# Steps of VectorE reordered and handed to ScalarE while a graph network builds its adjacency

## The chip, the cores and the metric

One core of one Trainium2 chip runs the whole program. The metric is the time on the device for one execution, in microseconds (us). A core has engines that run side by side, each through its own list of instructions in order: TensorE (PE in the profile; its weight loads are PEld), VectorE (DVE), ScalarE (ACT), GpSimd (POOL) and SyncE (SP), which here only issues transfers. They wait for one another by semaphores.

## The reference

625 nodes with 256 features, 10,625 edges sorted by their end node `dst`. Two graph layers, each behind a layer norm and a ReLU, are added to x:

```
h = relu(layernorm(x))
for l in 0, 1, 2:                                   # edge convolution, mean over the incoming edges
    m = concat(h[dst], h[src] - h[dst]) @ W_l + b_l
    h = relu(segment_sum(m, dst) / max(count, 1))
x = x + concat(h, h1, h2, h3) @ Wf + bf
h = relu(layernorm(x));  a = segment_sum(edge_weight * (h @ W)[src], dst) + bias
x = x + relu(batchnorm(a) * gamma + beta)
```

All sums over edges go through two 625 x 625 matrices: the number of edges from s to d, and the sum of their weights. The first part of the kernel builds both; the rest multiplies by them.

## The kernel before, in words

**Tiles.** The edges are cut into 85 tiles of 125. For each tile t, `src_hot` (L583 on VectorE, L933 and L936 on ScalarE) is a one-hot matrix, 125 edges by 626 nodes: VectorE makes it in one comparison with `edge_cols`, ScalarE in two steps, the distance |node - src| and then relu(1 - distance). `dst_hot` holds, for 17 tiles at a time (a group c), the one-hot of the end nodes in a narrow window of 28: `plain_window` (L572) makes it, and `weighted_window` (L579) multiplies it by the high and the low part of the scaled edge weights (`weight_parts`). As the edges are sorted, the window moves with the tile.

**Placing.** TensorE takes the tiles in order and multiplies `src_hot` of a tile (its weights, 128 nodes s at a time) by the tile's window (L1272). The results are block r of the end nodes (125 of them), in five banks, one for each block s of source nodes. Block 0 is done piece by piece, five matmuls a tile, and between its pieces stand other jobs at fixed places (L1276 to L1292): `turn_h0(b)` turns the normalized rows of node block b, `turn_vecs` turns the bias vectors, `neighbour_terms_0` multiplies h by W0's lower half. The dictionary `jobs` (L1250) says before which piece each `turn_h0` stands. The blocks 1 to 4 go in two halves: the first half of the pieces for the banks s = 0 to 4, then the second half for the banks. In front of the first half of bank s, TensorE waits for `parts_copied` of block r - 1, bank s (L1297), that is for ScalarE to have emptied the bank. Behind block 0 come the rest of `neighbour_terms_0`, behind block 1 `own_terms_0` (L1189, four results that ScalarE reads), behind block 2 and inside block 4 the row counts (`sum_counts`, L1244). Then come `sums_0` and the layers. Block r uses the tiles 0 to 18, 15 to 35, 32 to 52, 49 to 69 and 66 to 84. Its second half begins with tile 9, 25, 42, 59 or 75.

**Who makes which tile.** `SCALAR_EARLY`, `SCALAR_NEXT` and `SCALAR_LATER` (L65) name the tiles of ScalarE: 0 and 4 before the normalization, 22 and 27 among the normalized rows, and 34 and 38, 52, 71 behind its copies of block 0, 1 and 2. The other 77 are VectorE's, in order, in the loop from L622; `src_hot` has 36 slots, so that tile t waits for the placing of tile t - 36. Other work of VectorE stands at fixed tiles of the loop: the next group's windows two tiles before a group ends (L628), the copy of the bias vectors and the cast of `degree_r` at `VECS_AT`, the low parts u_lo at 30, 38 and 42, the difference of W0's halves at 33, the flag at 62.

**The first steps.** TensorE turns the edge rows and weight rows into columns, in the banks "edges", "weights" and "parts". VectorE takes from them `rel` (L565, the end node within its window), `edge_cols` (L567) and `weight_parts` (L604). L606 to L614 reduce to `dev_max`: how far an edge lies outside its window, and whether the two parts give the weight exactly; if not, a slow general way is taken later. Then come the statistics of x (L536, L542), `weighted_window(0)`, and `scale_shift` (L545: reciprocal, shift) once ScalarE has taken the root (L921). ScalarE turns x, scale and shift into the normalized rows h0 (L967) and copies their turned form out (`h0_high`).

**ScalarE's list** from L991 on: for every block r, five times two copies (`copy_block`, L977: counts, and the two parts of the weights), between them the high parts u_hi and `own_terms`, and behind the block its tiles of `SCALAR_LATER[r]`. `high_part` casts a weight matrix to its high part: wb1 behind block 1 (L1008), wf1 behind block 3 (L1011), wb2 behind block 4. GpSimd subtracts for the low part of wf1 and wb2. Ten matmuls on zeros (`keep_warm(10)`, L1153) fill TensorE's time before the first tile.

**Transfers.** SyncE issues the weight loads in a fixed order, three of the later ones behind the own terms and behind low parts; ScalarE issues weights and x at the start, and its share of the output at the end.

Of the kernel before, what the change touches and what calls it, by code (L numbers as in the profile page):

```python
# [34 lines left out]
ALU = mybir.AluOpType  # L35
# [7 lines left out]
KF = D // P  # L43
# [21 lines left out]
SCALAR_EARLY, SCALAR_NEXT, SCALAR_LATER = (0, 4), (22, 27), {0: (34, 38), 1: (52,), 2: (71,)}  # L65
SCALAR_TILES = SCALAR_EARLY + SCALAR_NEXT + sum(SCALAR_LATER.values(), ())
VECS_AT, DIFF_AT = 13, 33
# [87 lines left out]
def gnn_kernel(nc, x, src, dst, edge_weight, W0, b0, W1, b1, W2, b2, Wf, bf, W4, b4, gamma, beta, out):  # L155
    with ExitStack() as ctx:
# [224 lines left out]
        groups.plan(["parts"], weight_parts_ready, 2)  # L381
# [126 lines left out]
        def _(dve):  # L508
# [58 lines left out]
            dve.tensor_copy(edge_cols[:, :, :], e2).then_inc(edge_cols_ready, 1)  # L567
# [24 lines left out]
            def low_rows(name, b, done, n=1):  # L592
# [8 lines left out]
            groups.wait_filled(dve, "parts")  # L601
            p3 = groups.bank["parts"][0:EP, 0:3 * TILES].rearrange("p (v t) -> p v t", v=3)
            p2 = groups.bank["parts"][0:EP, 0:2 * TILES].rearrange("p (v c j) -> p c v j", v=2, c=NB)
            dve.tensor_copy(weight_parts[:, :, :, 0:PER], p2).then_inc(weight_parts_ready, 1)  # L604
            dve.wait_ge(weight_cols_ready, 1)
            dve.scalar_tensor_tensor(out=dev[:, 1, :], in0=parts_f[:, 0, :], scalar=WEIGHT_SCALE, in1=p3[:, 2, :],  # L606
                                     op0=ALU.mult, op1=ALU.not_equal).then_inc(weight_parts_ready, 1)
            step.add(dve.scalar_tensor_tensor(out=dev[:, 0, :].rearrange("p (c j) -> p c j", c=NB), in0=rel[:, :, 0:PER],
                                              scalar=-(WINDOW - 1) / 2, in1=window_scale[:, :, :], op0=ALU.add,
                                              op1=ALU.mult))  # L610
            step.wait()
            dve.wait_ge(weight_parts_ready, 2)
# [6 lines left out]
            weighted_window(0)  # L619
            scale_shift(range(NB), norm_ready)  # L620
            dve.wait_ge(edge_cols_ready, 1)
            for t in range(TILES):  # L622
                if t == VECS_AT:
                    groups.wait_filled(dve, "vecs")
                    dve.wait_ge(constants_ready, 4)
                    dve.tensor_copy(vecs[:, :], groups.bank["vecs"][:, 0:6 * KF]).then_inc(vecs_ready, 1)
                    dve.tensor_copy(degree_r[:, :], degree_f[:, :]).then_inc(degree_ready, 1)
# [274 lines left out]
        def _(act):  # L902
# [10 lines left out]
            nc.scalar.activation(row_parts[:, 0, :], weight_rows[:, :], ACT.Copy, scale=WEIGHT_SCALE).then_inc(row_high_ready, 1)  # L913
            groups.wait_filled(act, "weights")
# [77 lines left out]
            for r in range(NB):  # L992
                for s in range(NB):
# [6 lines left out]
                    if r == 1 and s >= NB - 2:  # L1000
                        if s == NB - 2:
                            act.wait_ge(vecs_ready, 1)
                        own_terms(0, (0,) if s == NB - 2 else (1, 2, 3))
# [4 lines left out]
                if r == 1:  # L1008
                    act.wait_ge(raw_loaded[1], 16)
# [484 lines left out]
```

## Time and profile before

| | us |
|---|---|
| median of 3 runs (lowest, highest) | 112.17 (111.88, 112.23) |
| the profiled execution: its time | 112.24 |
| its span, from the first instruction to the last | 110.4 |
| busy: PE, PEld | 100.4 (91%), 92.3 (84%) |
| busy: VectorE, ScalarE, GpSimd | 87.9 (80%), 62.3 (56%), 16.6 (15%) |
| granted TensorE clock, mean | 0.99 |

The profile is of one execution. Its times count from the first instruction, so the time of the execution is 1.8 us longer than the span. A row of a timeline gives start, length, engine, line, operation, operands and, behind x, how many instructions are merged in it; in square brackets stands the idle time of the engine before it and who ended it. The length of an instruction overlaps with the next: what one costs its engine is the distance from its start to the next start. An engine's share of the span is a mean over stages with different limits.

### The profile page before, as it was taken

To read this page: it belongs to the slowest core of one execution; us is meant where nothing else is said; L and a number is where in the kernel's file an instruction comes from. 1 tells how busy PE (TensorE), PEld (TensorE's weight loads), DVE (VectorE), ACT (ScalarE), POOL (GpSimd) and SP (SyncE) were. 2 spreads that over 40 slices of the span, in tenths; PEclk is the share of its full clock that TensorE was granted. 3 is DMA by queue.
4 is the path that set the end of the run, shared out by engine and by line. 5 is a ranking of instruction groups with operands and counts; after the bars stand their busy time and mean duration, and the time that the engine had idled before them with its cause. 6 is when DMAs were issued, how large, how long until landed. Compare 5 with 4: busy or idle time off the path is not lost.

```text
span 110.4 us, 2688 instructions
## 1 busy us (share of the span) xinstructions
PE 100.4 (91%) x1040; PEld 92.3 (84%) x1040; DVE 87.9 (80%) x259; ACT 62.3 (56%) x151; POOL 16.6 (15%) x24
## 2 busy tenths in 40 slices
PE   0398999799999999999999999999999999999940
PEld 0334998787898989989999999999999999999730
DVE  2599999999999998999934599831999989627860
ACT  1596999997797964312858035557323245241640
POOL 7200000000000076000092800490000000000000
PEclk9999999999999999999999999999999999999995
DMA  1879710000110000000143000000000000000035
GB/s 32 246 214 201 261 46 0 0 6 3 42 59 0 6 6 3 6 0 3 23 167 98 3 0 0 0 6 0 0 6 0 0 0 0 0 0 6 0 88 147
DMA packets 5401, 4.63 MB, mean 42 GB/s; under 512 B 555, under 2 KB 5386, under 8 KB 5386
## 3 DMA queue, kind: packets, MB, share of 16 engines
q1 hardware_dynamic: 4460, 3.68, 11.5%
q10 hardware_dynamic: 926, 0.75, 2.6%
q8 instruction: 10, 0.16, 0.7%
q14 instruction: 5, 0.04, 0.1%
HBM read 3.79 MB, written 0.64 MB: 40 GB/s over the span
## 4 chain that ended last, share of the span: by engine, by line
PE 60%; DVE 28%; DMA 5%; issue 2%; ACTq 1%; DVEq 0%
DVE src_hot L583 17%; PE bank L1373 14%; PE bank L1122 11%; PE bank L1124 11%; PE bank L1123 11%; PE bank L1272 5%; DMA x_in<-in_x_dram 5%; PE bank L1206 4%; PE bank L1411 2%; PE bank L1351 2%; DVE stats L536 2%; DVE u_lo L596 1%; DVE dst_hot L579 1%; DVE dst_hot L572 1%; DVE stats L853 1%
## 5 line engine op out<-in xcount | busy, mean ns | idle before, releaser
L583 DVE TENSOR_SCALAR src_hot<-node_id,edge_cols 125x626 f16<-125x626 f16 x77 | 23.5, 381 | 0.0
L1272 PEld LDWEIGHTS bank<-dst_hot,src_hot 125*128 125x128 f16 x505 | 19.0, 98 | 3.4 <-DVE src_hot L583 1.7
L1272 PE MATMUL bank<-dst_hot,src_hot 125*128 125x84 f16 (+6 forms) x505 | 20.3, 195 | 1.3 <-DVE src_hot L583 0.9
L1373 PE MATMUL bank<-counts,u_lo 125*128 125x312 f32 (+3 forms) x60 | 16.7, 309 | 0.0
L1048 ACT ACTIVATE h_hi<-pre 128x312 fp32r<-128x312 f32 (+1 forms) x12 | 5.6, 466 | 16.9 <-DVE pre L746 16.9
L1373 PE MATMUL bank<-counts,u_hi 125*128 125x312 f32 (+3 forms) x48 | 14.0, 307 | 0.0
L487 POOL TENSOR_TENSOR parts<-parts 125x625 f32<-125x625 f32 x5 | 6.4, 1299 | 43.0 <-DVE src_hot L583 35.9
L1373 PEld LDWEIGHTS bank<-counts,u_lo 125*128 125x128 f32 (+1 forms) x60 | 11.0, 189 | 0.0
L988 ACT ACTIVATE parts<-bank 125x250 f32<-125x250 f32 x25 | 10.2, 410 | 0.0
L762 DVE TENSOR_TENSOR weights_lo<-bank,weights_hi 125x500 fp32r<-125x500 f32 (+1 forms) x7 | 3.9, 617 | 7.0 <-ACT weights_hi L907 7.0
L1373 PEld LDWEIGHTS bank<-counts,u_hi 125*128 125x128 f32 (+1 forms) x48 | 9.1, 189 | 0.0
L949 ACT ACTIVATE own<-bank,vecs 128x312 f32<-128x312 f32 (+1 forms) x12 | 6.3, 523 | 4.1 <-PE bank L1124 3.1
L1122 PE MATMUL bank<-wf_hi,h_hi 128*125 128x256 f32 x30 | 8.4, 281 | 0.0
L1123 PE MATMUL bank<-wf_hi,h_lo 128*125 128x256 f32 x30 | 8.4, 281 | 0.0
L1124 PE MATMUL bank<-wf_lo,h_hi 128*125 128x256 f32 x30 | 8.4, 281 | 0.0
L746 DVE TENSOR_TENSOR pre<-pre,own 128x312 f32<-128x312 f32 (+1 forms) x12 | 6.7, 558 | 0.4
L907 ACT ACTIVATE counts<-bank 125x125 fp32r<-125x125 f32 x20 | 5.8, 292 | 1.7 <-PE bank L1272 1.7
L742 DVE TENSOR_TENSOR pre<-bank,inv_count 128x312 f32<-128x312 f32 (+1 forms) x12 | 5.7, 478 | 1.3 <-PE bank L1373 1.3
L933 ACT ACTIVATE distance<-node_id,edge_cols 125x626 f16<-125x626 f16 x8 | 6.6, 830 | 0.1
L907 ACT ACTIVATE u_hi<-bank 125x256 fp32r<-125x256 f32 (+1 forms) x13 | 5.2, 416 | 2.5 <-PE bank L1124 2.5
L1122 PE MATMUL bank<-weights_hi,u_hi 125*128 125x312 f32 (+1 forms) x20 | 6.4, 318 | 0.0
L596 DVE TENSOR_TENSOR u_lo<-bank,u_hi 125x256 fp32r<-125x256 f32 (+1 forms) x13 | 5.6, 463 | 0.9 <-ACT u_hi L907 0.9
(146 smaller groups left out, 251.9 us busy)
## 6 DMA issues: line engine op xcount, KB each, us to landing
raw<-in_L_gnn_W_dram SPq DMA_DIRECT2D x3, 512.0 KB, 6.9
x_in<-in_x_dram ACTq DMA_DIRECT2D x1, 560.0 KB
raw<-in_L_gnn_Wf_dram SPq DMA_DIRECT2D x1, 512.0 KB, 3.8
out_dram<-x_in SPq DMA_DIRECT2D x2, 168.0 KB
wf<-in_L_gnn_Wf_dram SPq DMA_DIRECT2D x1, 256.0 KB, 7.8
raw<-in_L_gnn_Wf_dram SPq DMA_DIRECT2D x1, 256.0 KB, 2.6
raw<-in_L_gnn_W_dram SPq DMA_DIRECT2D x1, 256.0 KB, 4.1
out_dram<-x_in SPq DMA_DIRECT2D x2, 112.0 KB
```

Of the source, the lines that this page charges most:

```text
L487: pool.tensor_tensor(part[:, :, 0, :], part[:, :, 0, :], part[:, :, 1, :], ALU.add).then_inc(weights_summed, 1)
L583: dve.tensor_scalar(src_hot[:, t % RING, 0:IDS], node_id[:, 0:IDS], edge_cols[:, 0, t:t + 1], None, ALU.is_equal).then_inc(src_hot_vector, 1)
L596: dve.tensor_tensor(u_lo[0:BLK, b:b + n, :], rows, u_hi[0:BLK, b:b + n, :].bitcast(F32), ALU.subtract).then_inc(u_lo_ready, n)
L746: dve.tensor_tensor(pre_t[:, f, a:e], pre_t[:, f, a:e], own[:, f, a:e], ALU.add).then_inc(z_ready, 1)
L907: copy = lambda o, i: nc.scalar.activation(o, i, ACT.Copy)
L933: nc.scalar.activation(distance[:, :], node_id[:, 0:IDS], ACT.Abs, bias=edge_cols[:, 0, t:t + 1], scale=-1.0).then_inc(distance_ready, 1)
L988: nc.scalar.activation(parts[:, r, s, :, :], built[s][0:BLK, 1:KINDS, 0:BLK], ACT.Copy, scale=1.0 / WEIGHT_SCALE).then_inc(parts_copied, 1)
L1122: pe.matmul(o, lh, rh, start=start, stop=False)
L1123: pe.matmul(o, ll, rh, start=False, stop=False)
L1124: return pe.matmul(o, lh, rl, start=False, stop=stop)
L1272: return pe.matmul(built[s][:, :, n0:n0 + n], src_hot[:, t % RING, BLK * s:BLK * s + P], dst_hot[:, c, :, j // 2, c0:c0 + n, j % 2], start ...
L1373: ins = pe.matmul(bank[KF * h + f][:, 0:e - a], u[0:n, k, P * f:P * (f + 1)], counts[0:n, k, a:e], start=False, stop=(k == NB - 1 and u is ...
```

## The change

VectorE's first steps come in another order: `weighted_window(0)` moves before the statistics, the weights' check and its maximum behind it, and `scale_shift` into the loop in front of tile 3 (`SHIFT_AT`). ScalarE takes over the copies `edge_cols` and `weight_parts`, the cast `degree_r`, and tile 75. The cast of wb1 moves between the own terms, that of wf1 behind block 4. `VECS_AT` goes from 13 to 15, the jobs of block 0 stand two pieces later, and there is one warm-up matmul fewer. The bank "parts" is given back by `dev_ready`.

```diff
--- before.py
+++ after.py
@@ -62,9 +62,9 @@
 EPS = 1e-5
 
 FULL = 112
-SCALAR_EARLY, SCALAR_NEXT, SCALAR_LATER = (0, 4), (22, 27), {0: (34, 38), 1: (52,), 2: (71,)}
+SCALAR_EARLY, SCALAR_NEXT, SCALAR_LATER = (0, 4), (22, 27), {0: (34, 38), 1: (52,), 2: (71, 75)}
 SCALAR_TILES = SCALAR_EARLY + SCALAR_NEXT + sum(SCALAR_LATER.values(), ())
-VECS_AT, DIFF_AT = 13, 33
+SHIFT_AT, VECS_AT, DIFF_AT = 3, 15, 33
 U_AT = (30, 38, 42)
 FLAG_AT = 62
 
@@ -378,7 +378,7 @@
         groups.spare = (5, 6, 7)
         groups.plan(["edges"], edge_cols_ready, 1)
         groups.plan(["weights"], weight_cols_ready, 1, banks=(7,))
-        groups.plan(["parts"], weight_parts_ready, 2)
+        groups.plan(["parts"], dev_ready, 1)
         groups.plan([("h0", b) for b in range(2)], h0_t_ready, 1, banks=(7, 5))
         groups.plan(["vecs"], vecs_ready, 1, banks=(6,))
         groups.plan([("h0", 2)], h0_t_ready, 3, banks=(7,))
@@ -564,7 +564,6 @@
             dve.wait_ge(padding_ready, 2)
             dve.tensor_tensor(rel[:, :, 0:PER], e2[:, 1, :].rearrange("p (c j) -> p c j", c=NB),
                               base_id[:, :, 0:PER], ALU.subtract).then_inc(rel_ready, 1)
-            dve.tensor_copy(edge_cols[:, :, :], e2).then_inc(edge_cols_ready, 1)
 
             def plain_window(c):
                 ids = pair_id[:, :, :].unsqueeze(1).to_broadcast([EP, PAIRS, WINDOW, 2])
@@ -598,33 +597,30 @@
 
             dve.wait_ge(rel_ready, 1)
             plain_window(0)
-            groups.wait_filled(dve, "parts")
-            p3 = groups.bank["parts"][0:EP, 0:3 * TILES].rearrange("p (v t) -> p v t", v=3)
-            p2 = groups.bank["parts"][0:EP, 0:2 * TILES].rearrange("p (v c j) -> p c v j", v=2, c=NB)
-            dve.tensor_copy(weight_parts[:, :, :, 0:PER], p2).then_inc(weight_parts_ready, 1)
-            dve.wait_ge(weight_cols_ready, 1)
-            dve.scalar_tensor_tensor(out=dev[:, 1, :], in0=parts_f[:, 0, :], scalar=WEIGHT_SCALE, in1=p3[:, 2, :],
-                                     op0=ALU.mult, op1=ALU.not_equal).then_inc(weight_parts_ready, 1)
             step.add(dve.scalar_tensor_tensor(out=dev[:, 0, :].rearrange("p (c j) -> p c j", c=NB), in0=rel[:, :, 0:PER],
                                               scalar=-(WINDOW - 1) / 2, in1=window_scale[:, :, :], op0=ALU.add,
                                               op1=ALU.mult))
+            dve.wait_ge(weight_parts_ready, 1)
+            weighted_window(0)
+            dve.wait_ge(weight_cols_ready, 1)
+            step.add(dve.scalar_tensor_tensor(out=dev[:, 1, :], in0=parts_f[:, 0, :], scalar=WEIGHT_SCALE,
+                                              in1=groups.bank["parts"][0:EP, 2 * TILES:3 * TILES], op0=ALU.mult,
+                                              op1=ALU.not_equal))
             step.wait()
-            dve.wait_ge(weight_parts_ready, 2)
             dve.tensor_reduce(dev_max[:, :], dev[:, :, :].rearrange("p v t -> p (v t)"), AX.X, ALU.max,
                               apply_absolute_value=True).then_inc(dev_ready, 1)
             dve.wait_ge(x_loaded, 32)
             for b in range(NB):
                 moments_of(b)
             variances(range(NB))
-            weighted_window(0)
-            scale_shift(range(NB), norm_ready)
             dve.wait_ge(edge_cols_ready, 1)
             for t in range(TILES):
+                if t == SHIFT_AT:
+                    scale_shift(range(NB), norm_ready)
                 if t == VECS_AT:
                     groups.wait_filled(dve, "vecs")
                     dve.wait_ge(constants_ready, 4)
                     dve.tensor_copy(vecs[:, :], groups.bank["vecs"][:, 0:6 * KF]).then_inc(vecs_ready, 1)
-                    dve.tensor_copy(degree_r[:, :], degree_f[:, :]).then_inc(degree_ready, 1)
                 if t % PER == PER - 2 and t // PER + 1 < NB:
                     plain_window(t // PER + 1)
                     weighted_window(t // PER + 1)
@@ -911,6 +907,15 @@
             nc.scalar.activation(root_table[:, :], ident[0:1, 0:1], ACT.Sqrt)
             act.wait_ge(edge_weights_loaded, 16)
             nc.scalar.activation(row_parts[:, 0, :], weight_rows[:, :], ACT.Copy, scale=WEIGHT_SCALE).then_inc(row_high_ready, 1)
+            act.wait_ge(constants_ready, 4)
+            copy(degree_r[:, :], degree_f[:, :]).then_inc(degree_ready, 1)
+            act.wait_ge(rel_ready, 1)
+            copy(edge_cols[:, :, :], groups.bank["edges"][0:EP, 0:2 * TILES].rearrange("p (v t) -> p v t",
+                                                                                    v=2)).then_inc(edge_cols_ready, 1)
+            groups.wait_filled(act, "parts")
+            act.wait_ge(padding_ready, 1)
+            copy(weight_parts[:, :, :, 0:PER], groups.bank["parts"][0:EP, 0:2 * TILES].rearrange(
+                "p (v c j) -> p c v j", v=2, c=NB)).then_inc(weight_parts_ready, 1)
             groups.wait_filled(act, "weights")
             copy(parts_f[:, 0, :], groups.bank["weights"][0:EP, 0:TILES]).then_inc(weight_cols_ready, 1)
 
@@ -1000,18 +1005,20 @@
                     if r == 1 and s >= NB - 2:
                         if s == NB - 2:
                             act.wait_ge(vecs_ready, 1)
-                        own_terms(0, (0,) if s == NB - 2 else (1, 2, 3))
+                        if s == NB - 2:
+                            own_terms(0, (0,))
+                        else:
+                            own_terms(0, (1,))
+                            act.wait_ge(raw_loaded[1], 16)
+                            high_part(wb[1][0][:, :, :], raw[1][:, KF:2 * KF, :])
+                            own_terms(0, (2, 3))
                 for t in SCALAR_LATER.get(r, ()):
                     if t >= RING:
                         act.wait_ge(*last_half(t - RING))
                     source_tile(t)
-                if r == 1:
-                    act.wait_ge(raw_loaded[1], 16)
-                    high_part(wb[1][0][:, :, :], raw[1][:, KF:2 * KF, :])
-                if r == 3:
-                    act.wait_ge(raw_loaded[0], 32)
-                    high_part(wf1[0][:, :, :], raw[0][:, 0:KF, :])
-
+
+            act.wait_ge(raw_loaded[0], 32)
+            high_part(wf1[0][:, :, :], raw[0][:, 0:KF, :])
             act.wait_ge(raw_loaded[2], 16)
             high_part(wb[2][0][:, :, :], raw[2][:, KF:2 * KF, :])
 
@@ -1150,7 +1157,7 @@
             ins.then_inc(filled, 1)
             pe.wait_ge(constants_ready, 3)
             pe.wait_ge(padding_ready, 1)
-            keep_warm(10)
+            keep_warm(9)
 
             def turn_dev():
                 pe.wait_ge(dev_ready, 1)
@@ -1247,7 +1254,7 @@
                 return pe.matmul(o[:, 0:e - a], degree_r[0:rows, :], part[0:rows, NB - 1, a:e], start=opens, stop=closes,
                                  skip_group_check=True)
 
-            jobs = {2: (0,), 4: (1,), 6: (2,), 9: (3, 4)}
+            jobs = {4: (0,), 6: (1,), 8: (2,), 11: (3, 4)}
             assert max(jobs) < len(window_pieces(0))
             made = [0, 0]
 
@@ -1276,9 +1283,9 @@
                 if r == 0:
 
                     for i in range(len(pieces)):
-                        if i == 5:
+                        if i == 7:
                             turn_vecs()
-                        if i == 8:
+                        if i == 10:
                             neighbour_terms_0(U0_BLOCKS[:1])
                         for b in jobs.get(i, ()):
                             turn_h0(b)
```

## Rows read from the trace of the kernel before

**Rows 1.** The page, chain that ended last: shares of the span by engine.
```profile
PE 60%; DVE 28%; DMA 5%; issue 2%; ACTq 1%; DVEq 0%
```

**Rows 2.** Stretches: start:end, length, each engine's busy time, clock, DMA share, GB/s.
```profile
9.70:40.70 31.00, 29.76 (x555) 26.47 (x556) 30.79 (x96) 27.69 (x77) 1.31 (x2) 1.00 0.16 49
40.70:105.00 64.30, 64.28 (x461) 62.66 (x462) 49.10 (x124) 28.17 (x65) 12.58 (x11) 1.00 0.05 14
```

**Rows 3.** Timeline of VectorE, 4.9 to 13.3 us.
```profile
4.98 0.25 DVE L565 TENSOR_TENSOR rel<-bank,base_id 125x85 f16<-125x85 f32 x1 [0.40 <-PE bank L1141]
5.14 0.33 DVE L567 COPY edge_cols<-bank 125x170 f32<-125x170 f32 x1
...
5.71 0.33 DVE L604 CAST weight_parts<-bank 125x170 f16<-125x170 f32 x1
...
6.85 1.73 DVE L536 BATCH_NORM_STATS2 stats<-x_in 125x6 f32<-125x256 f32 x5
...
8.91 0.65 DVE L579 TENSOR_TENSOR dst_hot<-dst_hot,weight_parts 125x1008 f16<-125x1008 f16 x1
9.48 0.18 DVE L550 RECIPROCAL rstd<-rstd 125x5 f32<-125x5 f32 x1
9.70 0.17 DVE L552 SCALAR_TENSOR_TENSOR shift<-moments,rstd 125x5 f32<-125x5 f32 x1
9.78 3.31 DVE L583 TENSOR_SCALAR src_hot<-node_id,edge_cols 125x626 f16<-125x626 f16 x11
...
13.08 0.21 DVE L627 CAST degree_r<-degree_f 128x128 fp32r<-128x128 f32 x1
```

**Rows 4.** Timeline of ScalarE, 5 to 12 us.
```profile
5.26 0.24 ACT L907 ACTIVATE parts_f<-bank 125x85 f32<-125x85 f32 x1 [1.33 <-PE bank L1144]
5.50 0.82 ACT L933 ACTIVATE distance<-node_id,edge_cols 125x626 f16<-125x626 f16 x1
...
11.02 0.38 ACT L907 ACTIVATE h_t<-bank 128x250 f32<-128x250 f32 x1
```

**Rows 5.** Timeline of TensorE, 5 to 30 us.
```profile
5.41 4.22 PE L1134 MATMUL bank<-node_id,zeros_bf 125*128 125x512 f16 x10
...
22.21 2.06 PE L1272 MATMUL bank<-dst_hot,src_hot 125*128 125x54 f16 x47 [0.68 <-DVE src_hot L583]
```

**Rows 6.** Timeline of VectorE at tiles 33 to 37.
```profile
21.78 1.26 DVE L583 TENSOR_SCALAR src_hot<-node_id,edge_cols 125x626 f16<-125x626 f16 x4
```

**Rows 7.** Timeline of ScalarE, 21 to 31.3 us.
```profile
21.34 0.73 ACT L936 ACTIVATE src_hot<-distance 125x626 f16<-125x626 f16 x1
...
28.63 0.52 ACT L949 ACTIVATE own<-bank,vecs 128x314 f32<-128x314 f32 x1 [0.53 <-PE bank L1196]
...
30.52 0.61 ACT L907 ACTIVATE wb_hi<-raw 128x512 fp32r<-128x512 f32 x1
31.05 0.25 ACT L907 ACTIVATE counts<-bank 125x125 fp32r<-125x125 f32 x1
```

**Rows 8.** Timeline of ScalarE, 33 to 38 us.
```profile
33.29 0.89 ACT L933 ACTIVATE distance<-node_id,edge_cols 125x626 f16<-125x626 f16 x1
34.21 0.72 ACT L936 ACTIVATE src_hot<-distance 125x626 f16<-125x626 f16 x1
35.48 0.27 ACT L907 ACTIVATE counts<-bank 125x125 fp32r<-125x125 f32 x1 [0.54 <-PE bank L1272]
...
37.48 0.46 ACT L988 ACTIVATE parts<-bank 125x250 f32<-125x250 f32 x1
```

**Rows 9.** Timeline of TensorE's weight loads, 35 to 41 us.
```profile
35.26 2.92 PEld L1272 LDWEIGHTS bank<-dst_hot,src_hot 125*128 125x128 f16 x81 [0.20 <-DVE src_hot L583]
38.12 0.19 PEld L1247 LDWEIGHTS bank<-counts,degree_r 128*128 128x128 f32 x1
...
38.90 1.68 PEld L1272 LDWEIGHTS bank<-dst_hot,src_hot 125*128 125x128 f16 x50 [0.20 <-DVE src_hot L583]
```

**Rows 10.** Chain that ended last, in order of time, 38 to 41 us: start, length, what.
```profile
39.36 1.33 PE bank L1272 x41
```

## Prediction

> **What bounds the kernel now.** I read the page's chain first. TensorE and VectorE own nearly all of it, and ScalarE none [rows 1]: the reader sees that VectorE carries the chain until TensorE takes it over. The busy times by stretch then say where. From 40.7 us to 105 us TensorE is busy for 64.28 of 64.30 us, so an instruction that starts later or earlier at 40.7 moves the end by the same amount. The change can only matter before, where TensorE has 1.2 us of holes, VectorE is full, and ScalarE works 27.7 of 31 us [rows 2]. ScalarE is nearly full too, which no share of the whole span (56%) shows. So the question is what TensorE waits for between 9.7 and 40.7 us, and for whom the moved work is late.
>
> The execution profiled took 112.24 us around its span of 110.4, and the median of the runs is 112.17. The sum below is a difference, made in the profiled execution and added to the median. A measurement of this kernel can tell 0.3%, 0.34 us, from no change.
>
> **VectorE's first steps.** In front of the first normalization VectorE issues rel at 4.98, the edge copy at 5.14 and the weight copy at 5.71; the maximum ends at 6.71, and the statistics of x begin at 6.85, when x has landed [rows 3]. The edge and the weight copy are 0.33 long each, of which the next instruction covers 0.09: 0.24 each. Both go to ScalarE, and the weighted window (0.57 from 8.91 to the reciprocal at 9.48) comes to stand before the statistics. Now VectorE waits: parts leaves TensorE at 5.62, and ScalarE's copy of 170 numbers costs about 0.30 (estimate between 0.24 for 85 numbers and 0.38 for 250, [rows 4]), so the weighted window starts at about 5.99, the weights' check at 6.59, the maximum (which now waits for that check) at 6.87, and the statistics at 7.12 in place of 6.85. That is 0.27 late. The variances are then ready at 9.26, ScalarE's root at about 9.59, two tiles lie ahead of the shift (9.18 and 9.47), and the shift ends at 10.16 in place of 9.86 [rows 3]. Yet tile 3 starts at 10.07 in place of 10.36: VectorE is 0.29 ahead and everything behind the normalized rows on ScalarE is 0.29 behind. The degree cast saves VectorE 0.13 more (13.08 to 13.21), which makes 0.42 ahead, and from tile 75 on one tile more, 3.31/11 = 0.30.
>
> ScalarE pays four steps before x: the degree cast (0.2, in an idle stretch), the edge copy from 5.27, the weight copy from 5.65, then the old copy of row parts. Its tile 0 starts at about 6.0, in place of 5.50 [rows 4]. Tile 4 ends at 9.2, still before the variances at 9.26: this cover has 0.1 left, and if it is gone each tenth comes on top of the 0.29.
>
> **Block 0 and one warm-up fewer.** The ten warm-ups take 0.43 each [rows 5]; nine end at 9.28, and four pieces (in place of two) now lie ahead of the first turned row, which is 0.29 later. The work that goes in front is worth 2 x 0.14. I cost both edits together, and the moved jobs, at nothing: TensorE leaves block 0 at 16.6 as before. What hides them is the wait for the normalized rows. Ends: 0.1 better, 0.2 worse.
>
> **Block 1.** Before, TensorE waits here 0.68 until 22.21 for tile 33 [rows 5] and shortly for tile 35. VectorE makes 33, 35, 36, 37 from 21.78 on, 0.29 apart and 0.38 long [rows 6], so 35 ends at 22.45 and TensorE goes on at 22.50; with 0.42 of lead 33 is there at 21.74 and 35 at 22.03. But tile 34 is ScalarE's and ends at 21.34 + 0.73 = 22.07 [rows 7]; with the 0.29 it ends at 22.36. ScalarE has no idle time from 9.9 to there, so nothing swallows the delay. TensorE gets 34 at 22.40 and goes on at 22.44: a gain of 0.06 in place of the 0.4 that VectorE offers.
>
> **Block 2.** The own terms (24.1 to 28.5) are TensorE's own, and ScalarE waits for them 0.53 before the last [rows 7] and 0.50 before the one ahead; the copy of wb (0.61 long, 0.53 to the next start) now fills such a hole. So the copies of block 2 need not wait until 31.05. They start when TensorE has finished the first fifth of block 2, which in the old time is 30.85: with latency and the 0.06, at 30.83. Gain 0.22.
>
> **Tile 75 on ScalarE.** Five pairs of copies take 33.29 - 31.05 = 2.24, so tile 71 starts at 33.07. Tile 71 takes 34.94 - 33.29 = 1.65 [rows 8], and ends at 34.72. Then tile 75: 0.85 to the second step and 0.63 from there to the next instruction (0.72 less the usual overlap of 0.09), 1.48, without the slow first step that tile 71 had. The copies of block 3 so begin at 34.75 + 1.48 = 36.23, or 36.26 with the wait for the semaphore, where they began at 35.48 after 0.54 of idle time [rows 8]. They are 0.78 late. Who waits: TensorE opens each bank of block 4 when the copies of the same bank of block 3 are done. Before, the last of these ended at 37.94 and TensorE needed it at 38.12 [rows 8, 9]. Now it ends at 38.72: TensorE goes on at 38.75 in place of 38.12 to 38.14, 0.61 to 0.63 late. (The 0.2 spent for tile 69, and as much for 68 [rows 9], shrinks to some 0.3 in all, for nothing, as TensorE then stands at the first bank of block 4 at about 36.45 and waits 0.4 there.)
>
> The way back: VectorE's last tile, 84, ended at 39.30 and TensorE waited 0.20 for it [rows 9]: 41 of the 50 matmuls that begin at 38.90 follow at 39.36 [rows 10]. It now ends at 38.59, so this wait is gone. Sum: +0.61 - 0.20 = **+0.41 us**.
>
> By the rows, a tile costs VectorE 0.30 and ScalarE 1.48, five times as much [rows 3, 8]. The Trainium skill, "ScalarE: Activation LUTs" (Rules for kernel authors), says to put such simple operations on VectorE; by its figures (ACTIVATE with a pointer bias, then one without, less the overlap) the pair would be an estimated 1.42, and the sum 0.06 smaller.
>
> **What is hidden.** The casts of wf1 and wb2 at the end of ScalarE's blocks (0.6 more behind 41.9) stand before a wait for VectorE that ends at 44.7; if that cover went, h of layer 1 would be late. GpSimd's low part of wf1 starts 0.8 later than 41.9 and is used some 20 us on. No DMA moves queue; SyncE's issues hang on the own terms, as before. The bank of parts is freed by the maximum (7.2), well before the vectors are turned into it. The errors: start of ScalarE's chain 0.1, tile 75 0.1, block 0 0.2 the bad way and 0.35 the good way (below). The forecast's own range is 0.1 to 0.75 slower.
>
> **Rivals.**
> A. ScalarE is in time (ends faster). Place: the copies of block 3. If they still end by 38.1, the gains stay: 0.06 in block 1, about 0.2 of the waits on 68 and 69, 0.20 at tile 84, so -0.44 to -0.5. The point from which it decides: the first copy of block 3 at 35.6 or sooner. For it: ScalarE had 0.54 idle there and gets 0.22 more. Against: 1.48 is put on top, twice as much. Time 111.73, chance 0.18.
> B. The normalized rows are not late (no change). If root and shift come at the old time, tile 34 is no bound, and block 1 gains the full 0.4, which brings ScalarE's later chain forward as well: +0.41 - 0.35 = +0.06, 112.23. For it: two tiles of VectorE lie just where the root runs. Against: the 0.27 before x is added from five rows. Chance 0.17.
> C. TensorE's clock. The granted clock reads 1.00 up to 105 us [rows 2], yet the warm-ups come 0.43 apart, 512 columns at 1.2 per ns [rows 5], and the last is shorter than the others. With nine, and new holes of 0.2 to 0.45 among the first pieces, the rise may come later; then about 2 us of TensorE's work after 10.8 would take twice as long, less 0.4 that block 1's wait swallows: +1.6, 113.8. Chance 0.07. The Trainium skill, "TensorE: Matmul & The Clock Gate" (the HAM clock gate), says that the array runs at 1.2 GHz until it has been kept busy, and gives this pace for a cold array; by that rule, the pace is right and the recorded grant is not.
> D. The change does not do what it says: VectorE is no bound at all and tile 75 hides. Then nothing moves; this is within B's time, and I give it no chance of its own beyond 0.02.
>
> **The numbers.** Forecast 0.56, A 0.18, B with D 0.19, C 0.07. The forecast's 112.17 + 0.41 = 112.58. It falls above +0.34 in about two thirds of its range: slower 0.36 + 0.07 (C) + 0.02 (B's edge) = 0.45; same 0.20 + 0.17 (B and D) + 0.01 (A's edge) = 0.38; faster 0.17, the rest of A. The range runs from A's time to the forecast's upper end: 111.7 to 112.9, leaving out C and the tail of A below it.
>
> **What would show it.** Right: statistics at 7.1; shift at 10.15; tile 34 ready at 22.36 and a TensorE wait there; copies of block 3 from 36.2 with no idle time of ScalarE before them; holes of TensorE in front of the five banks of block 4, released by ScalarE's parts; VectorE's last tile at 38.6; the first sum at 41.1 in place of 40.72. Wrong: idle time of ScalarE before block 3's copies, a shift at 9.9, or placements of the first pieces at twice their pace.

## The result and the profile after

112.82 us (median of 6, 112.67 to 113.04) against 112.19 of the kernel before on the same chip: ratio 1.0051 (95% interval 1.003 to 1.0071). It is slower by 0.63 us.

| | before | after |
|---|---|---|
| profiled execution: time, span | 112.24, 110.4 | 113.04, 110.9 |
| first matmul (start) | 4.53 | 4.60 |
| first sum of layer 0 (end of the adjacency) | 40.72 | 41.42 |
| first sum less first matmul | 36.19 | 36.82 |
| first sum to last matmul | 65.75 | 65.78 |
| busy share, VectorE and ScalarE | 80%, 56% | 78%, 58% |

The profiled executions differ by 0.80 us. Of these 0.63 lie between the first matmul and the first sum, 0.07 before the first matmul, 0.03 between the first sum and the last matmul, and 0.07 behind it, where the span of the changed kernel ends sooner but the time lies further above the span (2.1 against 1.8). That the distance is the same 0.63 as that of the medians is partly chance: the six times of a kernel spread over 0.4 to 0.7 us, and the changed kernel's times lie 1.97 above their spans (median), against 1.82 for the kernel before in the later runs. I use the distance from first matmul to first sum below, since the first matmul of an execution comes anywhere from 4.45 to 4.69.

The page's chain; before it had no ScalarE in it [rows 1]:

```profile
PE 72%; ACT 12%; DVE 8%; DMA 3%; issue 2%; DVEq 0%; SPq 0%; ACTq 0%
```

VectorE's share fell from 28 to 8% and ScalarE came in with 12, although it is busy 58% of the span. The stretches that answer to [rows 2], in the same columns (the cut 0.7 later):

```profile
9.70:41.40 31.70, 29.98 (x551) 26.36 (x551) 31.43 (x96) 28.52 (x78) 2.55 (x2) 1.00 0.16 50
41.40:105.70 64.30, 64.28 (x461) 62.57 (x462) 47.70 (x122) 28.69 (x66) 11.38 (x10) 1.00 0.04 14
```

Behind the cut TensorE is as full as it was; ahead of it, it has 1.72 us of holes in place of 1.24. VectorE's timeline, which answers to [rows 3]:

```profile
5.05 0.25 DVE L565 TENSOR_TENSOR rel<-bank,base_id 125x85 f16<-125x85 f32 x1 [0.40 <-PE bank L1148]
...
6.07 0.68 DVE L578 TENSOR_TENSOR dst_hot<-dst_hot,weight_parts 125x1008 f16<-125x1008 f16 x1 [0.15 <-ACT weight_parts L903]
...
7.19 1.73 DVE L536 BATCH_NORM_STATS2 stats<-x_in 125x6 f32<-125x256 f32 x5
...
10.02 0.17 DVE L552 SCALAR_TENSOR_TENSOR shift<-moments,rstd 125x5 f32<-125x5 f32 x1
10.10 3.31 DVE L582 TENSOR_SCALAR src_hot<-node_id,edge_cols 125x626 f16<-125x626 f16 x11
```

Statistics and shift are later than before, tile 3 is earlier (10.10 against 10.36). ScalarE's timeline, which answers to [rows 4, 7 and 8]:

```profile
6.05 0.82 ACT L938 ACTIVATE distance<-node_id,edge_cols 125x626 f16<-125x626 f16 x1
...
21.71 0.73 ACT L941 ACTIVATE src_hot<-distance 125x626 f16<-125x626 f16 x1
...
30.90 0.28 ACT L903 ACTIVATE counts<-bank 125x125 fp32r<-125x125 f32 x1 [0.27 <-PE bank L1279]
...
33.18 0.90 ACT L938 ACTIVATE distance<-node_id,edge_cols 125x626 f16<-125x626 f16 x1
34.10 0.73 ACT L941 ACTIVATE src_hot<-distance 125x626 f16<-125x626 f16 x1
34.92 0.82 ACT L938 ACTIVATE distance<-node_id,edge_cols 125x626 f16<-125x626 f16 x1
35.77 0.72 ACT L941 ACTIVATE src_hot<-distance 125x626 f16<-125x626 f16 x1
36.41 0.26 ACT L903 ACTIVATE counts<-bank 125x125 fp32r<-125x125 f32 x1
...
38.40 0.45 ACT L993 ACTIVATE parts<-bank 125x250 f32<-125x250 f32 x1
```

The row at 36.41 has no bracket: ScalarE comes to the copies of block 3 straight from tile 75, at 36.41 in place of 35.48. And TensorE's weight loads, which answer to [rows 5 and 9]:

```profile
21.82 0.10 PEld L1279 LDWEIGHTS bank<-dst_hot,src_hot 125*128 125x128 f16 x1 [0.36 <-DVE src_hot L582]
22.49 1.71 PEld L1279 LDWEIGHTS bank<-dst_hot,src_hot 125*128 125x128 f16 x46 [0.57 <-ACT src_hot L941]
...
36.98 1.66 PEld L1279 LDWEIGHTS bank<-dst_hot,src_hot 125*128 125x128 f16 x36 [0.45 <-ACT parts L993]
38.90 0.19 PEld L1254 LDWEIGHTS bank<-counts,degree_r 128*128 128x128 f32 x1 [0.26 <-ACT parts L993]
39.12 0.36 PEld L1279 LDWEIGHTS bank<-dst_hot,src_hot 125*128 125x128 f16 x9
39.80 1.46 PEld L1279 LDWEIGHTS bank<-dst_hot,src_hot 125*128 125x128 f16 x50 [0.32 <-issue]
```

The reader sees the exchange: VectorE's waits before the counts (at 34.96 and 35.26 in the kernel before) are gone, and in their place stand two waits for `parts`, released by ScalarE. The chain in order of time shows whose they are (start, length, what):

```profile
34.10 0.73 ACT src_hot L941
...
34.92 0.83 ACT distance L938
...
35.77 0.72 ACT src_hot L941
36.50 0.17 ACT counts L903
...
38.58 0.28 ACT parts L993
38.86 0.04 issue
38.90 0.38 PE bank L1254
...
41.42 0.53 PE bank L1358 x2
```

### The profile page after: what moved, and what is told of

Same layout as the page of the kernel before. It is cut to its first block, busy times and chain, and to the rows that moved or that the text cites. A ratio compares the mean times of both kernels' runs of the same rounds, so it can differ in the third digit from the quotient of the medians.

```text
span 110.9 us, 2690 instructions
## 1 busy us (share of the span) xinstructions
PE 100.6 (91%) x1039; PEld 92.4 (83%) x1039; DVE 87.0 (78%) x255; ACT 64.3 (58%) x156; POOL 16.6 (15%) x24
## 4 chain that ended last, share of the span: by engine, by line
PE 72%; ACT 12%; DVE 8%; DMA 3%; issue 2%; DVEq 0%; SPq 0%; ACTq 0%
PE bank L1380 14%; PE bank L1129 11%; PE bank L1131 11%; PE bank L1130 11%; PE bank L1279 8%; PE bank L1213 4%; PE bank L1203 4%; ACT parts L993 4%; DMA edge_rows_i<-in_dst_dram 3%; PE bank L1418 2%; ACT distance L938 2%; ACT src_hot L941 2%; PE bank L1358 2%; PE bank L1192 2%; ACT counts L903 2%
## 5 line engine op out<-in xcount | busy, mean ns | idle before, releaser
L1279 PE MATMUL bank<-dst_hot,src_hot 125*128 125x84 f16 (+6 forms) x505 | 20.8, 195 | 1.6 <-DVE src_hot L582 0.5
L938 ACT ACTIVATE distance<-node_id,edge_cols 125x626 f16<-125x626 f16 x9 | 7.5, 836 | 0.2
L941 ACT ACTIVATE src_hot<-distance 125x626 f16<-125x626 f16 x9 | 6.5, 726 | 0.3
```

The source lines that it names most:

```text
L938: nc.scalar.activation(distance[:, :], node_id[:, 0:IDS], ACT.Abs, bias=edge_cols[:, 0, t:t + 1], scale=-1.0).then_inc(distance_ready, 1)
L941: nc.scalar.activation(src_hot[:, t % RING, 0:IDS], distance[:, :], ACT.Relu, bias=1.0, scale=-1.0).then_inc(src_hot_scalar, 1)
L1279: return pe.matmul(built[s][:, :, n0:n0 + n], src_hot[:, t % RING, BLK * s:BLK * s + P], dst_hot[:, c, :, j // 2, c0:c0 + n, j % 2], start ...
```

## The experiments

My theory: the change is a gain and a larger loss. The first steps bring VectorE ahead, tile 75 makes ScalarE late for block 4, and the rest (casts, jobs, warm-up, `VECS_AT`) does next to nothing. Rivals: the first steps cost time by themselves, as the normalized rows are late; or the warm-up and TensorE's clock take it; or the casts do. The results of all runs (ratio to the kernel before on the same chip, with its interval; "end" is the first sum less the first matmul in the one profiled execution, 36.19 before). The medians come from several chips, so runs are compared by their ratios:

| run | median us | ratio | end |
|---|---|---|---|
| the change | 112.82 | 1.0051 (1.003 to 1.0071) | 36.82 |
| t75_back | 111.65 | 0.9945 (0.9925 to 0.9966) | 35.70 |
| t75_only | 113.24 | 1.0082 (1.0058 to 1.0106) | 37.11 |
| casts_back | 113.01 | 1.0064 (1.0045 to 1.0083) | 36.94 |
| warm10 | 112.94 | 1.0055 (1.0034 to 1.0076) | 36.83 |
| start_only | 111.70 | 0.9934 (0.9909 to 0.9959) | 35.73 |
| rest_only | 112.26 | 0.9998 (0.9976 to 1.002) | 36.01 |
| block1_free | 111.82 | 0.9941 (0.9919 to 0.9962) | 35.72 |
| third_early | 112.28 | 0.9989 (0.9973 to 1.0004) | 35.94 |
| third_b | 112.52 | 1.0031 (1.0015 to 1.0046) | 36.41 |
| third_c | 111.75 | 0.9961 (0.9948 to 0.9974) | 35.43 |
| shift_first | 112.42 | 1.0026 (1.0003 to 1.0049) | 37.06 |
| shift_first_w11 | 112.21 | 0.9991 (0.9978 to 1.0005) | 36.28 |

**t75_back: the change without tile 75.**

```diff
-SCALAR_EARLY, SCALAR_NEXT, SCALAR_LATER = (0, 4), (22, 27), {0: (34, 38), 1: (52,), 2: (71, 75)}
+SCALAR_EARLY, SCALAR_NEXT, SCALAR_LATER = (0, 4), (22, 27), {0: (34, 38), 1: (52,), 2: (71,)}
```

> The changed kernel with tile 75 on VectorE again; all else of the change stays. Theory (ScalarE's chain: its copies of block 3 come late because tile 75 stands before them): the copies of block 3 begin at about 35.0, TensorE no longer waits for them, VectorE's lead is worth something at tiles 67 to 69 and 84, and the first sum starts 0.44 before that of the kernel before, at about 40.3; ratio to the kernel before 0.996, 1.1 us under the changed kernel. Rival 1 (the cost is in the first steps, which bring the normalized rows 0.3 late): the time stays that of the changed kernel, ratio 1.003 to 1.007. Rival 2 (the shorter warm-up): the same, ratio 1.003 to 1.007.

Measured: 1.2 us below the change by the ratios, and below the kernel before by 0.6%. Its weight loads at the same place:

```profile
37.73 0.19 PEld L1254 LDWEIGHTS bank<-counts,degree_r 128*128 128x128 f32 x1
37.95 0.36 PEld L1279 LDWEIGHTS bank<-dst_hot,src_hot 125*128 125x128 f16 x9
38.53 1.66 PEld L1279 LDWEIGHTS bank<-dst_hot,src_hot 125*128 125x128 f16 x50 [0.22 <-DVE src_hot L582]
```

No wait for `parts` is left; the counts come at 37.73 in place of 38.90. The wait for VectorE's last tile, 84, is back, and it stands inside the fifty loads, in front of the tenth (they take 1.66 in place of 1.46). On ScalarE the copies of block 3 start at 35.09:

```profile
35.09 0.28 ACT L903 ACTIVATE counts<-bank 125x125 fp32r<-125x125 f32 x1 [0.24 <-PE bank L1279]
```

It follows that one edit turns the sign of the whole change.

**t75_only: the kernel before with tile 75 alone.**

```diff
-SCALAR_EARLY, SCALAR_NEXT, SCALAR_LATER = (0, 4), (22, 27), {0: (34, 38), 1: (52,), 2: (71,)}
+SCALAR_EARLY, SCALAR_NEXT, SCALAR_LATER = (0, 4), (22, 27), {0: (34, 38), 1: (52,), 2: (71, 75)}
```

> The kernel before with one edit: tile 75 on ScalarE. Theory (ScalarE's chain): VectorE ends its tiles 0.3 earlier, but the copies of block 3 begin at about 36.55 in place of 35.48, and the first sum starts 0.7 to 1.0 later than in the kernel before; ratio 1.006 to 1.009, more than the whole change costs. Rivals 1 and 2 (first steps, warm-up): the tile hides and frees VectorE, 0.0 to 0.3 us faster, ratio 0.997 to 1.0.

Measured: 0.9 us above the kernel before, in the median and at the first sum (37.11 - 36.19 = 0.92), as expected. The two waits of the changed kernel stand here too:

```profile
37.25 1.66 PEld L1272 LDWEIGHTS bank<-dst_hot,src_hot 125*128 125x128 f16 x36 [0.16 <-ACT parts L988]
39.16 0.19 PEld L1247 LDWEIGHTS bank<-counts,degree_r 128*128 128x128 f32 x1 [0.25 <-ACT parts L988]
```

**start_only: the kernel before with the first steps alone** (the edits of `edge_cols`, `weight_parts`, `degree_r`, the order, `SHIFT_AT`, the bank; `VECS_AT`, jobs, casts, ten warm-ups and tiles as before).

```diff
-VECS_AT, DIFF_AT = 13, 33
+SHIFT_AT, VECS_AT, DIFF_AT = 3, 13, 33
...
-            weighted_window(0)
-            scale_shift(range(NB), norm_ready)
...
+                if t == SHIFT_AT:
+                    scale_shift(range(NB), norm_ready)
```

> The kernel before with the change's first steps alone: the three copies on ScalarE, the weighted window before the statistics, the shift in front of tile 3, the bank of parts freed by the maximum. Tile 75, casts, jobs, warm-ups and the place of the bias vectors stay as before. Theory (VectorE's lead is the whole gain, ScalarE's late rows cost only at tile 34): last tile of VectorE at 38.9, first sum 0.44 earlier than in the kernel before, the same as with the whole change less tile 75; ratio to the kernel before 0.9945 to 0.9965. Rival (the lead pays only together with the moved jobs and casts, which keep TensorE and ScalarE fed while the rows are late): ratio 0.998 to 1.0.

Measured: 0.7 us below the kernel before. Its loads show where the gain is taken and where it is not:

```profile
22.38 1.71 PEld L1280 LDWEIGHTS bank<-dst_hot,src_hot 125*128 125x128 f16 x46 [0.60 <-ACT src_hot L941]
...
32.40 5.25 PEld L1280 LDWEIGHTS bank<-dst_hot,src_hot 125*128 125x128 f16 x141
```

Block 1 still waits, now for ScalarE's tile 34; but from 32.40 on 141 loads run through. The kernel before stopped there twice for tiles of VectorE, at 35.26 [rows 9] and at 34.96:

```profile
34.96 0.10 PEld L1272 LDWEIGHTS bank<-dst_hot,src_hot 125*128 125x128 f16 x1 [0.20 <-DVE src_hot L583]
```

The late rows do not cost what the earlier tiles bring.

**rest_only: the kernel before with casts, jobs, nine warm-ups and `VECS_AT` = 15** (the edits of the casts are left out below).

```diff
-VECS_AT, DIFF_AT = 13, 33
+VECS_AT, DIFF_AT = 15, 33
...
-            keep_warm(10)
+            keep_warm(9)
...
-            jobs = {2: (0,), 4: (1,), 6: (2,), 9: (3, 4)}
+            jobs = {4: (0,), 6: (1,), 8: (2,), 11: (3, 4)}
```

> The kernel before with what is left of the change: two casts moved, jobs two pieces later, nine warm-ups, bias vectors at tile 15. Theory: nothing of this is on the path, since VectorE's last tile stays at 39.3; ratio 1.000 (0.998 to 1.002). Rival: the casts and jobs carry part of what the change gains, ratio 0.998 or less.

Measured: no difference; ten of twelve times lie between 112.10 and 112.43, two at 113.01 and 113.19 (see the last section). In the profiled execution the first sum comes 0.18 sooner than before (36.01 against 36.19), and so does VectorE's last tile; why is open.

**casts_back and warm10: the change with the casts of wb1 and wf1 where they were, and, as a kernel of its own, the change with ten warm-ups.** The cut shows what casts_back puts back for wb1.

```diff
+                if r == 1:
+                    act.wait_ge(raw_loaded[1], 16)
+                    high_part(wb[1][0][:, :, :], raw[1][:, KF:2 * KF, :])
```

> The changed kernel with the two casts where they were, wb1 behind block 1's copies and wf1 behind block 3's. Theory (ScalarE's chain): the cast of wb1 stands before the copies of block 2 again and pushes tiles 71 and 75 and the copies of block 3 by 0.15 to 0.25; first sum 0.2 later than in the changed kernel, ratio to the kernel before 1.007. Rivals 1 and 2: no difference to the changed kernel, 1.005.

> The changed kernel with ten warm-up matmuls in place of nine. Theory (ScalarE's chain): the first pieces start 0.43 later, before a wait for the normalized rows that hides it; no difference to the changed kernel, ratio to the kernel before 1.003 to 1.007. Rival 2 (shorter warm-up costs clock): 0.3 us or more faster than the changed kernel, ratio 1.002 or less, and the placements of the first pieces come closer together.

Measured: in time neither can be told from the change. By the profiles, warm10 ends as the change does (36.83 against 36.82), casts_back 0.12 later. Its cast of wb1 stands in front of the copies of block 2, with no idle time between:

```profile
30.38 0.61 ACT L903 ACTIVATE wb_hi<-raw 128x512 fp32r<-128x512 f32 x1
30.90 0.26 ACT L903 ACTIVATE counts<-bank 125x125 fp32r<-125x125 f32 x1
```

That is 26.45 behind its first matmul (4.45), against 30.90 - 4.60 = 26.30 in the change: the moved cast is worth 0.15 on ScalarE, which has no idle time from there to the last copy of block 3, and 0.12 at the first sum.

**block1_free: t75_back with tile 36 in place of 34 on ScalarE,** so that block 1 doesn't wait for ScalarE.

```diff
-SCALAR_EARLY, SCALAR_NEXT, SCALAR_LATER = (0, 4), (22, 27), {0: (34, 38), 1: (52,), 2: (71,)}
-SHIFT_AT, VECS_AT, DIFF_AT = 3, 15, 33
+SCALAR_EARLY, SCALAR_NEXT, SCALAR_LATER = (0, 4), (22, 27), {0: (36, 38), 1: (52,), 2: (71,)}
+SHIFT_AT, VECS_AT, DIFF_AT = 3, 15, 36
```

> The changed kernel with tile 75 on VectorE, and in block 1 the tiles that TensorE waits for early: the difference of W0 behind tile 35 in place of before 33, and ScalarE's tiles 36 and 38 in place of 34 and 38. Theory (the end is set by VectorE's last tile): TensorE leaves block 1 about 0.55 earlier, but waits in block 3 for tiles 66 to 69 again, and tile 84 is no earlier; first sum at 40.3 as without these edits, ratio to the kernel before 0.9935 to 0.9955. Rival (each wait of TensorE counts by itself): 0.5 us more off, ratio 0.990.

```profile
23.51 3.98 PEld L1203 LDWEIGHTS bank<-h_t,raw 128*128 128x128 f32 x16
...
34.67 0.10 PEld L1279 LDWEIGHTS bank<-dst_hot,src_hot 125*128 125x128 f16 x1 [0.20 <-DVE src_hot L582]
...
38.60 1.67 PEld L1279 LDWEIGHTS bank<-dst_hot,src_hot 125*128 125x128 f16 x50 [0.20 <-DVE src_hot L582]
```

The own terms begin at 23.51 in place of t75_back's 24.15, yet the first sum comes no sooner (35.72 against 35.70): VectorE's waits return, three of them from 34.4 to 35.0, and the counts come 33.12 behind the first matmul as against 33.10. The last fifty loads take 1.67 and 1.66, both with the wait for tile 84. With tile 75 back on VectorE, VectorE's last tile sets the end, and the wait in block 1 costs nothing.

**third_early, third_b, third_c: one more tile for ScalarE, but behind its copies of block 0,** where I took the copies that follow to have slack, so that VectorE's last tile comes 0.3 sooner. ScalarE reads the first own term sooner in all three, and the second one too in third_b and third_c; third_early and third_c take the tiles 36, 38, 40, then 53 and 71 (with `DIFF_AT` = 36), third_b takes 34, 36, 38, then 52 and 71. third_c also moves the cast of wb1 behind block 4. The lines are those of third_b, against t75_back:

```diff
-SCALAR_EARLY, SCALAR_NEXT, SCALAR_LATER = (0, 4), (22, 27), {0: (34, 38), 1: (52,), 2: (71,)}
+SCALAR_EARLY, SCALAR_NEXT, SCALAR_LATER = (0, 4), (22, 27), {0: (34, 36, 38), 1: (52,), 2: (71,)}
...
-                    if r == 1 and s >= NB - 2:
+                    if r == 1 and s in (0, 1, NB - 1):
```

> As the last kernel, and the further tile for ScalarE is taken where ScalarE has time: tiles 36, 38 and 40 behind block 0, 53 behind block 1, 71 behind block 2, and the first own term read two banks sooner. So VectorE has one tile less, as in the change, but block 3's copies have only tile 71 before them. Theory (it is the place of the tile and not ScalarE's added work that costs): VectorE's last tile at 38.6, first sum 0.7 earlier than in the kernel before and 0.3 earlier than with 75 on VectorE, ratio 0.991 to 0.993. Rival (ScalarE is full, and any tile more makes its chain late): ratio 0.997 or more.

> The change less tile 75, with tile 36 given to ScalarE instead (34, 36, 38 behind block 0), and the first two own terms read behind the copies of banks 0 and 1 of block 1. In the try with 36, 38, 40 the late reading of these two held TensorE for 0.75 (bank of the last own term) and 1.13 us (bank of the turned maximum). Theory (the tile costs only by what waits behind it, and here nothing does once the own terms are read in time): no such holes, VectorE's last tile at 38.6 and no wait for it, first sum at 40.1 or 0.2 under the change less tile 75; ratio to the kernel before 0.991 to 0.9935. Rival (ScalarE is full in any order): the copies of block 2 or 3 come late, ratio 0.996 or more.

> The same order of own terms on the try with 36, 38, 40 and 53, with W0's difference behind tile 35, and the cast of wb1 behind block 4. TensorE leaves block 1 at 23.5 and must not wait for own terms again. Theory: block 2 begins at about 27.9; ScalarE is now what it waits for in blocks 3 and 4 (0.3 to 0.7 us), first sum between 39.9 and 40.3, ratio 0.990 to 0.9945. Rival: as for the last kernel, 0.996 or more.

All three brought the end of VectorE's last tile to 34.0 behind the first matmul (34.3 in t75_back). The first two missed what I expected, each by a wait that I had not listed. third_early, then third_b:

```profile
27.08 0.83 PEld L1202 LDWEIGHTS bank<-h_t,raw 128*128 128x128 f32 x4 [0.75 <-ACT own L954]
29.03 0.08 PEld L1163 LDWEIGHTS bank<-ident,dev_max 125*1 125x1 f32 x1 [1.13 <-issue]
...
38.90 1.47 PEld L1278 LDWEIGHTS bank<-dst_hot,src_hot 125*128 125x128 f16 x50 [0.20 <-issue]
```

```profile
31.82 1.67 PEld L1279 LDWEIGHTS bank<-dst_hot,src_hot 125*128 125x128 f16 x45 [1.06 <-ACT src_hot L941]
```

In the first, TensorE's own terms wait 0.75 for a bank that ScalarE reads too late, and the turning of `dev_max` (the maximum of the first steps) waits 1.13. The profile names nobody for the second wait; that it is also for a bank which ScalarE had yet to read is my reading, and in third_c, which reads the first two own terms behind the copies of banks 0 and 1, the wait is gone. In third_b, tile 52 stands behind everything and is ready 1.06 too late. third_c avoids both. Its waits for ScalarE are 0.32 at an own term and 0.21 in block 3, and the first sum comes 35.43 behind the first matmul, 0.27 sooner than in t75_back and as expected. Yet its ratio, 0.9961, is no better, and is the number that I had put on the rival (a full ScalarE). Its times lie 2.26 above their spans (median), those of the kernel before 1.82 and of t75_back 1.84. Why this margin differs between programs stays open, and with it whether the third tile is worth anything.

**shift_first: t75_back with the shift ahead of the tiles.**

```diff
-SHIFT_AT, VECS_AT, DIFF_AT = 3, 15, 33
+SHIFT_AT, VECS_AT, DIFF_AT = 1, 15, 33
```

> The change less tile 75, with the shift before tile 1 in place of before tile 3, so that VectorE waits for ScalarE's root as before the change. Theory (VectorE's lead sets the end, the normalized rows' time does not): the normalized rows come 0.1 earlier, but VectorE stands idle for 0.45 us and its last tile is at 39.3 again; first sum at 40.75, ratio to the kernel before 0.998 to 1.001. Rival (the late normalized rows are the cost of the change, so bringing them forward pays): ratio 0.994 or less.

Measured: 1.0026, above what I expected, and two groups, seven times of 112.11 to 112.43 and five of 112.83 to 113.22. The profile (112.94) is of the second. VectorE waits for the root, as expected, and TensorE behind it runs at half its pace; I show VectorE, then TensorE:

```profile
9.61 0.19 DVE L550 RECIPROCAL rstd<-rstd 125x5 f32<-125x5 f32 x1 [0.44 <-ACT rstd L926]
```

```profile
9.17 0.38 PE L1279 MATMUL bank<-dst_hot,src_hot 125*128 125x42 f16 x5
10.36 1.02 PE L1279 MATMUL bank<-dst_hot,src_hot 125*128 125x60 f16 x15 [0.81 <-DVE src_hot L582]
11.19 0.66 PE L1170 MATMUL bank<-ident,h 125*128 125x125 f32 x2
11.64 0.73 PE L1279 MATMUL bank<-dst_hot,src_hot 125*128 125x60 f16 x10
```

That mixes two causes, so I parted them.

**shift_first_w11: the same with eleven warm-ups.**

```diff
-            keep_warm(9)
+            keep_warm(11)
```

> The last kernel (shift before tile 1, tile 75 on VectorE) with eleven warm-up matmuls in place of nine. In the last kernel's profile TensorE stood idle for 0.93 us before its second piece and then placed the pieces up to 13.6 us at half the pace (0.050 from matmul to matmul in place of 0.028), and 5 of its 12 executions lay 0.7 us above the other 7. Theory (this hole behind the shorter warm-up kept the clock down, and without it the kernel shows what the shift's place alone does): the pieces come at full pace, no group of executions 0.7 us higher, VectorE's last tile at 39.2 to 39.3, first sum at 40.6 to 40.8, ratio to the kernel before 0.997 to 1.001. Rival (the slow pace has nothing to do with the warm-up): again some executions in three 0.7 us higher, ratio 1.002 or more.

```profile
5.33 3.89 PE L1141 MATMUL bank<-node_id,zeros_bf 125*128 125x512 f16 x11
9.06 0.29 PE L1279 MATMUL bank<-dst_hot,src_hot 125*128 125x42 f16 x5
10.35 0.90 PE L1279 MATMUL bank<-dst_hot,src_hot 125*128 125x60 f16 x15 [1.01 <-DVE src_hot L582]
11.09 0.41 PE L1170 MATMUL bank<-ident,h 125*128 125x125 f32 x2
11.34 0.45 PE L1279 MATMUL bank<-dst_hot,src_hot 125*128 125x60 f16 x10
```

Measured: the second group is gone (none of twelve times, against five of twelve: few, but the profiles show the same), the pairs of L1170 take 0.41 in place of 0.66, and the end is 0.58 later than in t75_back. With TensorE at full pace, the place of the shift behind two tiles is worth about as much as all the first steps bring (36.19 - 35.73 = 0.46, in the medians 0.68).

## Why the prediction was right

It said 112.58, 0.41 above before; 112.82 was measured, 0.63 above, inside the range of 0.1 to 0.75 of the forecast itself. The mechanism was right; two terms of the sum were too small, by a third of the total.

- **First steps.** Statistics 7.12 expected, 7.19 measured; shift ended 10.16 and 10.19; tile 3 10.07 and 10.10; tile 0 of ScalarE 6.0 and 6.05. This execution began 0.07 later, so VectorE was on time or 0.04 early. start_only shows that this part is a gain.
- **Block 1.** Tile 34 ready at 22.36 expected, 21.71 + 0.73 = 22.44 measured, and TensorE waits for it until 22.49. The wait moved from VectorE to ScalarE, as said. block1_free adds what I had not seen: once VectorE sets the end, that wait costs nothing.
- **Copies of block 2.** 30.83 expected, 30.90 less 0.07 measured. Of the gain of 0.22 the cast's move has 0.15 (casts_back).
- **Tile 75.** Copies of block 3 at 36.26 expected with no idle time before them, 36.41 - 0.07 = 36.34 measured. The pair cost 36.41 - 34.92 = 1.49; I had 1.48 from the rows. By the figures of the Trainium skill, "ScalarE: Activation LUTs" (What ACT_TABLE_LOAD costs), the pair was an estimated 1.42, so the row was the nearer. The rule of the Trainium skill, "ScalarE: Activation LUTs" (Rules for kernel authors), to keep such simple work on VectorE agrees with the price of a tile, 0.30 on VectorE and 1.49 on ScalarE. That the tile cost 1.2 us in the end (t75_back) comes from its place in ScalarE's list, in front of the copies of block 3.
- **What was mis-sized.** Two terms. TensorE reaches the counts at 38.90 - 4.60 = 34.30 behind its first matmul, before at 38.12 - 4.53 = 33.59: +0.71 in place of +0.61 to 0.63, mostly tile 71 and the five pairs, 0.06 and 0.04 longer than added up. The second term was not in the sum. Between the nine loads behind the counts and the next fifty TensorE reads the flag that chooses the slow general way (L1317), and from start to start 39.80 - 39.12 = 0.68 go by, before 38.90 - 38.34 = 0.56: 0.12 more. The wait of 0.20 for tile 84 went as said (from the fifty to the first sum 41.39 - 39.80 = 1.59, before 40.69 - 38.90 = 1.79, by the starts of the loads). The rows give 0.71 + 0.12 - 0.20 = 0.63.
- **A row misread.** For the 0.20 of tile 84 the prediction names [rows 9], whose bracket stands in front of the fifty. But tile 84 ended at 39.30, behind their start at 38.90; its wait is the one in front of the 41 [rows 10]. The bracket belongs to the reading of the flag: third_early has the same 0.20, and 38.90 - 38.34 = 0.56, with no wait for tile 84 in its fifty loads (1.47). That both were 0.20 was luck. Nor does that wait hide the 0.12. The distance is 0.67 to 0.71 in the four kernels with tile 75 on ScalarE, all of which wait for `parts` in front of the counts, but 0.70 in third_c too, which doesn't; in the others it is 0.55 to 0.61. What sets it stays open.
- **Rivals.** A (ScalarE in time) fell: the copies began at 36.41, not by 35.6. Its price was right, though: without tile 75 the end is 0.49 sooner, and A had put 0.44 to 0.5 on it. B fell with the shift at 10.19 and the wait for tile 34. C fell for this change (only the pieces before 9.7 were slow, and warm10 changes nothing), but its mechanism is real, as shift_first shows; its price of 1.6 was not reached: in shift_first the late rise cost 37.06 - 36.28 = 0.78.

The best versions are the ones without tile 75: start_only at 0.9934, block1_free at 0.9941 and t75_back at 0.9945, which their intervals do not part. All three beat both kernels.

## What to carry to other kernels

Price a moved piece at the place where it comes to stand in the other engine's ordered list, against the slack of the next result that someone waits for: an engine busy 56% of the span had 0.72 us of slack there (0.54 idle before block 3's copies, and 0.18 between their end at 37.94 and TensorE's need at 38.12), and the tile cost 1.49. When a change is a bundle, run each part alone; here a gain of 0.5 to 0.7 and a loss of 1.2 stood behind a ratio of 1.005. Before work is handed to an engine with slack, list every consumer behind it: two of three attempts to give ScalarE one more tile elsewhere failed on a wait that I had not listed. And check that a bracket of idle time belongs to the wait that one wants to remove: compare when the awaited instruction ended with when the waiting one started.

## What the runs showed of the hardware

The granted clock reads 1.00 in every stretch from 4.5 us to 105 us, but the pace of the matmuls shows two levels and an instant of change that differs between executions. The 512-column warm-ups start 0.427 apart (512 columns at 1.2 GHz) and are 0.634 long each, the last two of third_c 0.379 long; the pair of L1170, which turns normalized rows, takes 0.66 at the slow level and 0.41 to 0.43 at the fast one. By the pace, the change came at about 8.2 us in third_c and 9.7 in the changed kernel, between 10.2 and 10.6 in t75_back, and in shift_first at about 14.0, where the own terms start at 25.58 in place of 24.31 in shift_first_w11 (both with the first matmul at 4.45). In shift_first_w11, where the warm-ups reached beyond the rise, 1.01 us without work for TensorE, ahead of the second piece, did not slow what followed. By the Trainium skill, "TensorE: Matmul & The Clock Gate" (the HAM clock gate), a cold array starts 512 columns 426.7 ns apart, and the recorded clock events can be wrong; the traces agree with both.

The kernels with nine warm-ups have rare executions 0.7 us above the rest: two of twelve in rest_only, one of twelve in third_b, five of twelve in shift_first. With ten it is one of 24 times of the kernel before, those measured beside rest_only. Only one of shift_first was profiled, so that a late rise is behind the others is argued, not shown.
